# Mixture of experts: first products of two experts together, then second products of two, with four hidden buffers

## Reference

```python
router_logits = flat @ router_w + router_b
router_probs = softmax(router_logits)
topk_probs, topk_idx = top_k(router_probs, 2)
weights = zeros.at[arange(T)[:, None], topk_idx].add(topk_probs)
shared_out = gelu(flat @ sw1 + sb1) @ sw2 + sb2
h1 = gelu(einsum('td,edh->teh', flat, rw1) + rb1)
expert_out = einsum('teh,ehd->ted', h1, rw2) + rb2
mixed = einsum('ted,te->td', expert_out, weights)
return layernorm(x + shared_out + mixed)
```

## Time and profile before

| | us |
|---|---|
| median of 3 runs | 3390.69 (3390.16 to 3393.29) |
| the profiled execution | 3390.42 |
| its span | 3388.4 |
| PE busy | 3214.6 (95%) |
| POOL busy | 2711.6 (80%) |
| DVE busy | 2327.5 (69%) |
| ACT busy | 1997.4 (59%) |
| mean granted clock of TensorE, share of full | 0.978 |

### The profile page before, as it was taken

One profiled execution on the slowest core, in us unless ns is written; L12 is line 12 of the kernel. 1 busy time (PEld: TensorE's weight loads), 2 busy tenths in 40 slices (PEclk: granted clock), 3 DMA queues, 4 the chain that ended last, 5 costly groups with the idle time before them and its releaser, 6 DMA issues. The chain is left out here.

```text
span 3388.4 us, 57253 instructions
## 1 busy us (share of the span) xinstructions
PE 3214.6 (95%) x20861; PEld 1941.9 (57%) x20861; DVE 2327.5 (69%) x3736; ACT 1997.4 (59%) x3829; POOL 2711.6 (80%) x1350
## 2 busy tenths in 40 slices
PE   5995898599999999999999999999999999998998
PEld 2553455355555555555555555555555555555898
DVE  4987797766666676667666667666666666664664
ACT  5983797355555555555655565555555555554454
POOL 1970585199999999999999999999999999996333
PEclk9997899799999999999999999999999999999999
DMA  2320221200000000000000000000000000000000
GB/s 52 100 88 13 65 88 55 70 1 1 4 4 1 4 1 4 1 4 1 4 5 1 7 7 7 1 4 1 4 4 1 4 1 2 1 1 23 20 26 10
DMA packets 63941, 58.90 MB, mean 17 GB/s; under 512 B 7722, under 2 KB 47220, under 8 KB 63604
## 3 DMA queue, kind: packets, MB, share of 16 engines
q1 hardware_dynamic: 61858, 54.88, 5.7%
q10 hardware_dynamic: 1810, 0.37, 0.1%
HBM read 48.41 MB, written 6.82 MB: 16 GB/s over the span
## 5 line engine op out<-in xcount | busy, mean ns | idle before, releaser
L1637 POOL TENSOR_TENSOR den_g<-den_g,p 128x1024 f32<-128x1024 f32 x888 | 2117.3, 2384 | 142.4 <-ACT p L1559 27.1
L1712 DVE TENSOR_REDUCE quarters<-psum 128x1 f32<-128x512 f32 x2004 | 1290.7, 686 | 647.4 <-PE psum L1085 602.8
L1559 ACT ACTIVATE p<-psum 128x512 f32<-128x512 f32 x2048 | 1084.4, 600 | 384.8 <-PE psum L1436 343.9
L1449 PE MATMUL psum<-p,v 128*64 128x512 f32 x4096 | 922.8, 592 | 0.0
L1449 PEld LDWEIGHTS psum<-p,v 128*64 128x64 f32 x4096 | 293.2, 137 | 582.0 <-issue 506.9
L1085 PE MATMUL psum<-k_main,q_main 64*128 64x512 f32 x2048 | 449.3, 424 | 6.9 <-DVE quarters L1092 5.6
L1436 PE MATMUL psum<-row_shift,row_ones 64*128 64x512 f32 x2048 | 416.5, 389 | 0.0
L1436 PE MATMUL psum<-q_main,k_main 64*128 64x512 f32 x2048 | 413.4, 391 | 2.2 <-PEq L1228 2.2
L1436 PE MATMUL psum<-q_main,k_rest 64*128 64x512 f32 x2048 | 415.2, 389 | 0.0
L1436 PE MATMUL psum<-q_rest,k_main 64*128 64x512 f32 x2048 | 415.0, 390 | 0.0
L719 POOL TENSOR_TENSOR fed_s<-dx,work 128x1024 f32<-128x1024 f32 x128 | 302.5, 2365 | 78.8 <-remote 60.0
(11 more groups left out here) (289 smaller groups left out, 3219.7 us busy)
## 6 DMA issues: line engine op xcount, KB each, us to landing
work<-bc_rows SPq DMA_DIRECT2D x128, 256.0 KB, 3.2
resid<-in_resid SPq DMA_DIRECT2D x8, 256.0 KB, 4.2
x_mid<-resid SPq DMA_DIRECT2D x8, 256.0 KB, 2.6
residual<-x_mid SPq DMA_DIRECT2D x8, 256.0 KB, 4.4
x<-x_mid SPq DMA_DIRECT2D x8, 256.0 KB, 2.8
out<-mixed SPq DMA_DIRECT2D x8, 256.0 KB, 2.3
w_qkv<-in_Wq SPq DMA_DIRECT2D x16, 64.0 KB, 1.9
w_qkv<-in_Wk SPq DMA_DIRECT2D x16, 64.0 KB, 2.0
```

The source lines that it names most:

```text
L1449: last = nc.tensor.matmul(o_bank[hi(h), :], vv[:, kt, hi(h)], p[:, u % LIVE, h, :], start=(kt == 0), stop=(kt == KT - 1))
L1559: nc.scalar.activation(p[:, u % LIVE, h, :], bank_of["score", u, h], ACT.Exp, scale=float(DH) ** -0.5).then_inc(p_ready, 1)
L1637: nc.gpsimd.tensor_tensor(sums, first, src, ALU.add).then_inc(added_g, 1)
L1712: nc.vector.reduce_max(quarters[:, to % 2, h, n:n + 1], bank_of["max", u, h], X_AXIS).then_inc(max_read, 1)
```

## The change

TensorE's order becomes: `up(0)`, `up(1)`, then for every even k: `up(k+2)`, `up(k+3)`, the extra work of k, `down(k)`; for every odd k only the extra work and `down(k)`. `hid` has four buffers instead of two, and a gelu waits for the `down` four steps back instead of two. The PSUM banks stay as they are: two pairs for `up`, two single ones for `down`, by the parity of k. The orders of ACT, DVE, POOL and SP are not changed.

```diff
-        hid = ph.sbuf("hid", [P, 2, HH, BANK])
+
+        HIDDEN = 4
+        hid = ph.sbuf("hid", [P, HIDDEN, HH, BANK])
...
-                                last = nc.tensor.matmul(dst, hid[:, k % 2, h, j * P:(j + 1) * P], down_w[:, e, h, :],
+                                last = nc.tensor.matmul(dst, hid[:, k % HIDDEN, h, j * P:(j + 1) * P], down_w[:, e, h, :],
...
                     up(0)
+                    up(1)
                     for k, (u, e) in enumerate(steps):
-                        if k + 1 < len(steps):
-                            up(k + 1)
+                        if k % 2 == 0:
+                            for ahead in range(k + 2, min(k + 4, len(steps))):
+                                up(ahead)
...
-                        if k >= 2:
-                            act.wait_ge(down_psum, k - 1)
+                        if k >= HIDDEN:
+                            act.wait_ge(down_psum, k - HIDDEN + 1)
                         for h in range(HH):
-                            nc.scalar.activation(hid[:, k % 2, h, :], up_bank(k)[:, h * BANK:(h + 1) * BANK], ACT.Gelu,
+                            nc.scalar.activation(hid[:, k % HIDDEN, h, :], up_bank(k)[:, h * BANK:(h + 1) * BANK], ACT.Gelu,
```

## The result

The changed kernel takes 3408.79 us (median of 5 runs, 3407.71 to 3409.9); the kernel before took 3390.95 (5 runs). The ratio is 1.0051, 95% interval [1.004, 1.0062]: about 18 us slower, 3411.3 was forecast.

What follows compares the result with a forecast made beforehand. TensorE was taken as the bound, busy throughout a steady group, so any wait is paid in full. Stream and T gains of 2.8 us each against new waits and clock falls summed to +20.9 on 3390.42: 3411.3 us, range 3398 to 3421.

Steps and rivals of the forecast that it cites:

- stream, 35 switches: TensorE's matmul stream: 35 fewer `up` follow a `down`, each first matmul 0.08 us cheaper, -2.8 us.
- share, odd groups: Groups 1, 3, 5: the next group's step 1 `up` waits 3.42 us for gelu 8 behind ACT's `share`, +10.3 us.
- share, even groups: Groups 4 and 6: the next group's step 1 `up` waits 0.34 us for gelu 8 behind `share`, +0.7 us.
- square after odd groups: Groups 2, 4, 6: step 4's `up` waits 1.30 us for gelu 2, behind ACT's square, +3.9 us.
- square after even groups: Groups 1, 3, 5, 7: step 4's `up` waits 1.51 us for gelu 2, behind ACT's square, +6.0 us.
- R in group 0: R directly follows step 4's `down` in group 0, losing the cover of one `up`: +1.47 us.
- T in groups 0 and 2: Step 6's T is covered by two `up` instead of one: -1.38 us each, -2.8 together.
- clock: TensorE's clock falls to half behind each of three 3.42 us waits, 1.36 us each: +4.1 us, bounds 0 and 13.6.
- What the order does to the waits: TensorE's new order makes `up` wait for gelus that in-order ACT holds behind `share` and `square_act`.
- Theory B: From the experiments: pairs of results overload DVE and POOL, so the time is lost wherever one looks.
- rival (c): ACT loads the exponential's table while waiting for `biased`; odd share waits 1.28 us shorter, no clock fall: 3402.7 us, chance 0.08.
- The estimate of 3428: Whole-kernel time if ACT's table loads had the skill page's drain, making `share` 2.8 us longer in seven groups.

Runs made afterwards that it cites:

- e3: Changed kernel with DVE's bias of step 5 ahead of that step's part and ACT's square behind gelu 2 instead of gelu 1: 3388.92 us, ratio 0.9997.
- e1: Changed kernel with DVE's bias of step 5 put ahead of the part of step 5: 3398.74 us, ratio 1.0023.
- e2: Changed kernel with ACT's square of the previous group moved from behind gelu 1 to behind gelu 2: 3400.14 us, ratio 1.0022.
- e5: Changed kernel with step 7's `down` put between the next group's `up` of steps 0 and 1, in groups 1, 3 and 5: 3400.19 us, ratio 1.0025.
- e11: Changed kernel with an extra, long satisfied semaphore wait ahead of ACT's wait for `biased` in `share`: 3417.40 us, ratio 1.0072.
- e7: Changed kernel with eight unused filler matmuls between the next group's `up` of steps 0 and 1, in groups 1, 3 and 5: 3406.28 us, ratio 1.0045.
- e6: Changed kernel with an extra, long satisfied semaphore wait behind ACT's wait for `biased` in `share`: 3409.04 us, ratio 1.0051.
- e8: Changed kernel with two hidden buffers instead of four: 3419.74 us, ratio 1.0083.
- e4: Kernel before, its order kept, with only `hid` four deep and the gelu waiting four steps back: 3391.29 us, ratio 0.9998.
- e9: Changed kernel with both moves of e3 and DVE's rest of x at step 4 behind the attention's add: 3388.58 us, ratio 0.9991.

## Why the prediction was right, and where it was wrong

The direction, the places and the total held; several terms were off, and they partly cancelled. Term by term, in us of the last phase:

| term | forecast | measured |
|---|---|---|
| stream, 35 switches | -2.8 | about -0.5 (0.12 in two groups, e3) |
| share, odd groups | 3 x 3.42 = 10.3 | 3 x 2.18 = 6.5 |
| share, even groups | 0.7 | 0 (groups 4 to 5: 31.17 in changed, 31.16 in e1) |
| square after odd groups | 3 x 1.30 = 3.9 | 3 x 0.96 = 2.9 |
| square after even groups | 4 x 1.51 = 6.0 | 4 x 1.42 = 5.7 |
| R in group 0 | 1.5 | 1.4 by the idle time (2.07 - 0.70) |
| T in groups 0 and 2 | -2.8 | -2.8 (1.65 to 0.28 by starts) |
| clock | 4.1 | 3 x 1.6 = 4.8 |
| sum | 20.9 | 18.0; the last phase says 18.0 |

The measured terms have errors of some tenths together, so the exact agreement of the sum is chance; no cost of more than that is missing.

- **What the order does to the waits** was right: e1, e2 and e5 each took away the waits they aimed at, and e3 took back the whole loss. Theory B fell with them.
- **Share: the step that failed** is "from the first table load to the start of gelu 8, 2.84", counted from `biased`. The first load does not wait for `biased`, so 1.28 is hidden. This was rival (c), which had got 0.08; the evidence against it was the load of group 0, read without asking which of the gelu's two waits it had waited for. The same 1.28 removes the even groups' 0.34; e11, which holds the load, brings both back.
- **Rival (c)** also said that the clock would then hold. That was its own error: with waits of 1.86 the falls came anyway. The forecast of three falls was right in number by luck: they were taken for the three U1', and one of them came at R instead.
- **Square** was mis-sized by 0.1 after an even group and by 0.3 after an odd one. A square and a gelu overlap by 0.1 (3206.26 to 3206.79, not 0.63), and after an odd group the pair of `down` covers 3.49 instead of 3.40. The rest, some 0.15, I did not take apart.
- **The stream: failed.** -2.8 rested on the record of one matmul's start. Measured from step 8 to step 8 of whole groups it is nearly 0.
- **The total** was nearer than its parts: the odd groups' share was 3.8 too high and the stream's gain 2.3 too large, and these two errors have opposite signs.
- **The estimate of 3428** for longer table loads does not follow from its own terms: 2.8 in each of seven groups is 19.6, not 16.7. Nothing else hangs on it; in changed a load takes 1.28 and gelu 8 starts 0.02 behind it (3190.71 and 3192.01).
- **The clock.** The price was right (1.4 forecast, 1.6 measured by e7 and by the stretches above), the condition not: I put it at waits between 2.68 and 3.55. In the last phase it fell behind R's 2.07 in eight of nine profiles, behind R's 1.47 in the one, behind U1' at 1.86 in four of nine waits (changed, e2, e6), at 2.37 in two of three (e8), at 3.20 in two of three (e11), behind U4' at 1.15 or less never. Behind the 1.49 at T in groups 0 and 2 it did not fall in four waits (before, e4), though it fell behind 1.47 at R. So the length of the wait does not decide alone; what does, here, stays open.

## What to carry to other kernels

When matmuls are regrouped, go through every wait in the queues of the other engines and ask what stands behind it: here two waits that had been harmless for ACT became TensorE's, because the products that cover them fell from five to two for `share` and from eight to five for the square. Moving two instructions (DVE's bias ahead of one part, ACT's square behind one more gelu) cost nothing that shows and gave all of it back. Price a seam over a whole period of the loop, not by one instruction's recorded start.

## What was not expected of the hardware

- With one semaphore wait ahead of an ACTIVATE, its ACT_TABLE_LOAD ran before that wait ended; with two, it was held by the one written second (e6 and e11: a load behind gelu 7, or 4.96 us idle before it, 1.34 us on each critical wait). Whether this is how the program is compiled or what the chip does, no run here shows.
- The clock of TensorE fell to 1.2 GHz for some 3.3 us behind an idle of only 1.47 us (e9, at R), and it did not behind one of 3.20 (e11, group 5).
